# Splitting query and key projections: a whole copy by ScalarE and the first subtraction on GpSimd

## The chip, the cores and the metric

The kernel runs on one core of one Trainium2 chip. The metric is the device time of one execution in microseconds (us). The engines are called as in the profile: PE (TensorE; PEld are its weight loads), DVE (VectorE), ACT (ScalarE), POOL (GpSimd) and SP (SyncE, which issues most DMAs).

## The reference

A transformer layer in float32 on `x` of 16 items of 512 tokens and 256 features. After a layer norm `xn`, the output is `x + attention(xn) + experts(xn)`.

```
q, k = low_rank_proj(xn, q_a, q_b), low_rank_proj(xn, k_a, k_b)     # 16 heads of 16
att  = softmax(causal(q k^T / 4));  y = att v;  attention = y @ o_w.T + o_b
experts: 8 experts, each takes its top 128 tokens of an item by gate probability,
         silu(x_in w1) w2, scaled by the gate and added to their rows
```

## The kernel before, in words

The low-rank factors are folded into one weight per side at the start. To keep float32 accuracy with bf16 matmuls, every query and key projection is split into three bf16 parts (first, middle, last), whose sum is the f32 value. The parts are stacked by DMA into `qstk` and `kstk` (six DMAs per side and item, one per term of the product), so that one bf16 matmul of 96 rows gives a score.

The attention stage runs over 16 items; each item has four slots (`g` = 0 to 3, four heads each), and each slot ten units `t` = 0 to 9. `slot_steps(b, g)` writes one common order of steps by hand, from the tables `SUMS` and `PROJECTIONS`; an entry (t, kind, ahead, k) puts a step for item b + ahead into unit t, behind that unit's score work. Every engine walks the same list and does its own part of each step, in order, so a step that waits holds up all behind it on that engine. Semaphores with counted values join the engines. Two items form the body of a loop; the first pair and the last are written out, with `prologue_steps` ahead.

In unit t of slot G, PE makes the transposed scores `scoret` of slot G+1 (line 887, two PSUM banks in turn) and the scores of slot G+3 (line 866, three banks). ACT takes exp of `scoret` (565), POOL masks the diagonal (469), and DVE takes row maxima of the scores (719). The value products of slot G, `pv` (908), come in units 2 and 5; the first needs all ten masks made during the slot before, and PE waits there. In slot 1 the first scores of the next item begin; PE waits for that item's twelve stacking DMAs (863).

A projection for item b+2 has steps `qk_first` and `qk` (three matmul passes each, 776), k = 0, 1 for the queries and 2, 3 for the keys. Its bank is one of two `SHARED` banks, used in turn in the order of the units and freed by a counter `shared_done`. Then:

- ACT copies the bank to bf16 as the first part (537).
- DVE subtracts the first part from the bank into `rest`, f32 in SBUF, and frees the bank (`take_low`, 588; called at 695). `rest` has two buffers.
- In step `mid`, ACT copies `rest` to bf16 as the middle part (541), POOL subtracts it from `rest` into the last part (460), and behind k=1 and k=3 SP issues the six DMAs of a side (400).

`mid` of k=3 stands in the next item's slot 0 at t=1 (ahead 1), those of k=0, 1, 2 in slot 3. POOL's other work in the order: adding the output bias to `xres` in slot 2 at t=1 (477), which waits for that transfer, and small steps of the layer norm. Behind the attention stage comes the expert stage (from line 963), which the change leaves alone.

Of the kernel before, what the change touches and what calls it, by code (L numbers as in the profile page):

```python
# [5 lines left out]
B, T, D = 16, 512, 256  # L6
# [19 lines left out]
def unit_parts(t, transposed):  # L26
# [5 lines left out]
    for h, i in parts:  # L32
# [12 lines left out]
     (9, "qk_first", 2, 1)],  # L45
    [(0, "qk", 2, 1), (0, "mid", 2, 0), (1, "mid", 2, 1), (4, "qk_first", 2, 2), (6, "qk", 2, 2), (8, "mid", 2, 2),
     (8, "qk_first", 2, 3), (9, "qk", 2, 3)])

SUMS = (
# [6 lines left out]
def slot_steps(b, g):  # L56

    G = GB * b + g  # L60
    put = {t: [] for t in range(UN)}
    for t, kind, ahead, k in SUMS[g]:
        if G + ahead < NG:
            put[t].append((kind, G + ahead, k))
    last_values = b == B - 2
    if last_values and g == 0:
        put[0].append(("v", b + 1, 0))
        put[1].append(("v", b + 1, 1))
        put[3].append(("v", b + 1, 2))
        put[4].append(("v", b + 1, 3))  # L70
    for t, kind, ahead, k in PROJECTIONS[g]:
        if last_values and kind == "v":
            continue
        if 0 <= b + ahead < B and (kind, b + ahead) != ("mid", 1):
            put[t].append((kind, b + ahead, k))
    for t, step in routing_steps(G):
        put[t].append(step)
    out = []
    for t in range(UN):
        out += [("scoret", G + 1, t)] * (G + 1 < NG) + [("score", G + 3, t)] * (G + 3 < NG) + put[t]  # L80
    return out
# [28 lines left out]
def prologue_steps():  # L110

    foldt = lambda n: [("foldt", n, half) for half in range(2)]
    qk = lambda b, mt: [("qk_first", b, mt), ("qk", b, mt)]
    out = [("xload", 0, 0), ("lnstat", 0, 0), ("lnstat", 0, 1), ("lnapply", 0, 0), ("xload", 1, 0)]

    out += foldt(0) + [("fold", 0, 0)] + foldt(1) + [("xt", 0, 0), ("xt", 0, 1), ("fold", 1, 0)]
    out += foldt(2) + qk(0, 0) + foldt(3) + qk(0, 1)
    out += [("mid", 0, 0), ("fold", 2, 0), ("mid", 0, 1), ("fold", 3, 0), ("wv", 0, 0), ("wv", 1, 0)]
    out += [("lnstat", 1, 0), ("lnstat", 1, 1)] + qk(0, 2) + qk(0, 3)
    out += [("mid", 0, 2), ("v", 0, 0), ("mid", 0, 3), ("v", 0, 1), ("v", 0, 2), ("lnapply", 1, 0), ("v", 0, 3)]  # L120
    out += [("xt", 1, dt) for dt in range(DT)] + [("wo", dt, 0) for dt in range(DT)] + [("ob", 0, 0)]
    for t in range(UN):
        out.append(("score", 0, t))
        if t in (0, 2, 4, 6):
            out += qk(1, t // 2)
        if t in (2, 4, 6):
            out.append(("mid", 1, t // 2 - 1))
    for t in range(UN):
        out += [("score", 1, t)] + [("maxt", 0, 0)] * (t == 2) + [("maxd", 0, 0)] * (t == 3) + [("mid", 1, 3)] * (t == 4)
    for t in range(UN):  # L130
        out += [("scoret", 0, t), ("score", 2, t)] + [("maxt", 1, 0)] * (t == 3) + [("maxd", 1, 0)] * (t == 4)
    return out
# [28 lines left out]
def build(nc, x, q_a, q_b, k_a, k_b, v_w, v_b, o_w, o_b, choice_w, w1, w2, out):  # L161
    fp32, f32r, bf16 = mybir.dt.float32, mybir.dt.float32r, mybir.dt.bfloat16
    i32, u32 = mybir.dt.int32, mybir.dt.uint32
    ALU, ACT, AX = mybir.AluOpType, mybir.ActivationFunctionType, mybir.AxisListType
# [5 lines left out]
                                            "rankt", "rowst")]  # L170
    unit_of = {s: n for n, s in enumerate(shared)}

    split_of = {s: n for n, s in enumerate(s for s in shared if s[0] in ("fold", "wv", "wo", "xt", "qk", "yt"))}
    U_PAIR, S_PAIR = 48, 16
    for i in range(1, PAIRS - 2):
        for s, z in zip(pair_steps(i), pair_steps(i + 1)):
            assert s not in unit_of or unit_of[z] - unit_of[s] == U_PAIR
# [9 lines left out]
    with ctx:  # L187
        def sem(name):
            return ctx.enter_context(nc.semaphore(name))
# [28 lines left out]
        with ExitStack() as mem:  # L218
# [67 lines left out]
            shared_done = [sem(f"shared_done{u}") for u in range(2)]  # L286
            hi_done = sem("hi_done")
            mid_done = sem("mid_done")
            lo_done = sem("lo_done")
            stacked = [sem(f"stacked{u}") for u in range(2)]  # L290
            logit_done = sem("logit_done")
# [54 lines left out]
            def bank_of(step):  # L346
                return unit_of[step] % 2
# [5 lines left out]
            def emptied(step, at):  # L353

                return at(unit_of[step] // 2 + 1, U_PAIR // 2)
# [67 lines left out]
            def _(pool):  # L423
# [15 lines left out]
                def steps(todo, at):  # L439
                    for step in todo:  # L440
                        kind, n, k = step
                        if kind == "gather":
                            if n == 0:
                                pool.wait_ge(gate_step, GATED + RANK_OPS + 3)
                                pool.wait_ge(xn_stored, 16 * B)
                            gather(nc, moe, xn_dram, n)
                        elif kind == "lnstat" and k == 1:

                            pool.wait_ge(mv_done, at(n + 1, 2))
                            if n >= 1:  # L450
                                pool.wait_ge(xn_done, at(n, 2))
                            nc.gpsimd.tensor_tensor(vareps[:], meanvar[:, :, 1], eps[:], ALU.add).then_inc(vareps_done, 1)
                            pool.wait_ge(vareps_done, at(n + 1, 2))
                            nc.gpsimd.tensor_tensor(rstd[:], vareps[:], mhalf[:], ALU.pow).then_inc(rstd_done, 1)
                        elif kind == "mid":

                            pool.wait_ge(mid_done, at(GB * n + k + 1, 2 * GB))
                            if n >= 1:
                                pool.wait_ge(stacked[(n - 1) % 2], at(STACK_DMAS * ((n - 1) // 2 + 1), STACK_DMAS))
                            nc.gpsimd.tensor_tensor(qk_part[2][:, k, :], rest[k % 2][:], qk_part[1][:, k, :],  # L460
                                                    ALU.subtract).then_inc(lo_done, 1)
                        elif kind == "scoret":

                            pool.wait_ge(exp_done, at(UN * n + k + 1, 8 * UN))
                            pool.sem_inc(pool_past1, 1)
                            cols = [col // P for _, _, col, _ in unit_parts(k, True)]
                            unit = probs[n % 2][:, 512 * k:512 * k + 512].rearrange("p (a c) -> p a c", c=P)
                            block = unit[:, 0:1, :] if len(cols) == 1 else unit[:, 0:cols[1] + 1:cols[1], :]
                            nc.gpsimd.affine_select(out=block, in_=block, compare_op=ALU.is_ge, fill=0.0, base=0,  # L469
                                                    pattern=[[0, len(cols)], [1, P]], channel_multiplier=-1)\  # L470
                                .then_inc(causal_done, 1)
                        elif kind == "xres":
                            pool.wait_ge(xres_in, at(16 * (n + 1), 32))
                            if n == 0:
                                bias = ("ob", 0, 0)
                                pool.wait_ge(shared_done[bank_of(bias)], emptied(bias, at))
                            nc.gpsimd.tensor_tensor(xres[:], xres[:], ob_all[:].unsqueeze(1).to_broadcast([P, TT, D]),
                                                    ALU.add).then_inc(xres_done, 1)
# [4 lines left out]
            def _(act):  # L483
# [15 lines left out]
                def steps(todo, at):  # L499
                    for step in todo:  # L500
# [32 lines left out]
                        elif kind == "qk":  # L533
                            act.wait_ge(shared_ready[p], filled(step, at))
                            if n >= 1 and k == 0:
                                act.wait_ge(stacked[(n - 1) % 2], at(STACK_DMAS * ((n - 1) // 2 + 1), STACK_DMAS))
                            nc.scalar.activation(qk_part[0][:, k, :], src[:], ACT.Copy).then_inc(hi_done, 1)
                        elif kind == "mid":
                            qk = ("qk", n, k)
                            act.wait_ge(shared_done[bank_of(qk)], emptied(qk, at))  # L540
                            nc.scalar.activation(qk_part[1][:, k, :], rest[k % 2][:], ACT.Copy).then_inc(mid_done, 1)  # L541
                        elif kind == "v":
                            act.wait_ge(shared_ready[p], filled(step, at))
# [30 lines left out]
            def _(dve):  # L574
# [9 lines left out]
                def take_low(step, at, low, whole, high):  # L584

                    p = bank_of(step)
                    dve.wait_ge(hi_done, split(step, at))
                    nc.vector.tensor_tensor(low, whole, high, ALU.subtract).then_inc(shared_done[p], 1)

                def steps(todo, at):  # L590
                    for step in todo:
# [97 lines left out]
                            take_low(step, at, xt_lo[:, k, :], src[:], xt_hi[:, k, :])  # L689
                        elif kind == "yt":  # L690
                            take_low(step, at, yt_lo[:, k, :], src[:], yt_hi[:, k, :])
                        elif kind == "qk":
                            if 4 * n + k >= 2:
                                dve.wait_ge(lo_done, at(4 * n + k - 1, 8))
                            take_low(step, at, rest[k % 2][:], src[:], qk_part[0][:, k, :])
                        elif kind == "ob":

                            dve.wait_ge(weights_in, N_WEIGHTS)
# [483 lines left out]
```

## Time and profile before

| | |
|---|---|
| median of 3 runs | 1292.59 us (1291.87 to 1296.5) |
| profiled execution | 1295.71 us, of which the span of the trace is 1293.8 us |
| busy PE, DVE, ACT, POOL | 92%, 75%, 52%, 53% of the span |
| PE's granted clock | 0.969 of full speed, mean |

The attention stage lies from about 54 us to 850 us, the expert stage behind it. A busy time is the share in which an engine had an instruction running; the waits say which event ended an idle stretch. As each engine works in the order of one list, the place of a wait in that order says more than the share.

### The profile page before, as it was taken

The numbers are of one execution on the slowest core, as the hardware profiler recorded it, in microseconds if no ns is written. First come the engines' busy times: TensorE is split into PE (matmuls) and PEld (weight loads), VectorE is DVE, ScalarE is ACT, GpSimd is POOL, SyncE is SP. The second block draws the span as 40 slices with busy tenths as digits, with TensorE's granted clock in tenths as the row PEclk, the third lists the DMA queues.
The fourth block names the chain that finished last, engine by engine and source line by source line (L and its number), as shares of the span: only waits on it lengthen the run. The fifth ranks groups of instructions, "written<-read, shape, count | busy, mean of one in ns | idle before, by whom it ended". The sixth has DMA issues, their size and how long they took to land. (4 is left out here: it accounts for less than half of the span.)

```text
span 1293.8 us, 29459 instructions
## 1 busy us (share of the span) xinstructions
PE 1184.1 (92%) x8502; PEld 819.8 (63%) x8502; DVE 967.2 (75%) x3293; ACT 668.7 (52%) x1312; POOL 692.0 (53%) x1021
## 2 busy tenths in 40 slices
PE   6799999999999999999999998769999999999995
PEld 5545555555555555555555553348988888888885
DVE  3588888879889888888888879935666666666662
ACT  2357667667667677677667665522332323233320
POOL 1235344355355355345345443344888888888885
PEclk9779999999999999999999999979999999999998
DMA  5443443443443443443444342132555555556454
GB/s 141 114 116 83 116 116 100 116 116 98 115 115 98 115 115 99 115 115 100 113 115 112 100 99 67 34 114 38 111 99 95 114 93 102 94 100 109 85 78 53
DMA packets 106287, 130.31 MB, mean 101 GB/s; under 512 B 21580, under 2 KB 75476, under 8 KB 106196
## 3 DMA queue, kind: packets, MB, share of 16 engines
q1 hardware_dynamic: 76356, 94.46, 28.1%
q0 software_dynamic: 24576, 33.57, 15.6%
q10 hardware_dynamic: 5264, 1.32, 0.5%
q8 instruction: 27, 0.44, 0.1%
q14 instruction: 64, 0.52, 0.1%
HBM read 44.84 MB, written 33.55 MB: 61 GB/s over the span
## 5 line engine op out<-in xcount | busy, mean ns | idle before, releaser
L719 DVE CUSTOM_DVE_ANT_0 junk<-bank,rowmask 128x256 bf16<-128x256 f32 (+3 forms) x1024 | 454.9, 485 | 60.3 <-PE bank L866 38.0
L565 ACT ACTIVATE probs<-bank 128x512 f32<-128x512 f32 x640 | 377.3, 598 | 158.0 <-PE bank L887 143.8
L469 POOL TENSOR_SCALAR_AFFINE_SELECT probs<-probs 128x256 f32<-128x256 f32 (+1 forms) x640 | 224.2, 363 | 311.0 <-ACT probs L565 308.9
L866 PE MATMUL bank<-kstk,qstk 96*128 96x256 bf16 (+3 forms) x1024 | 250.7, 306 | 34.3 <-DVE rowmax L719 17.3
L887 PE MATMUL bank<-qstk,kstk 98*128 98x256 bf16 (+3 forms) x1024 | 251.0, 307 | 3.8 <-ACT probs L565 2.6
L1049 POOL DMA_INDIRECT out_rows<-mixed,rows x128 | 208.9, 1632 | 58.2 <-issue 38.1
L1078 ACT ACTIVATE hid<-bank 128x512 f32<-128x512 f32 x128 | 76.6, 598 | 228.5 <-PE bank L1141 228.5
L908 PE MATMUL bank<-probs,vaug 128*32 128x512 f32 (+3 forms) x2048 | 168.5, 448 | 6.6 <-POOL probs L469 6.6
L1157 PE MATMUL bank<-w_hi,hid_hi 128*128 128x256 f32 x512 | 147.3, 288 | 0.0
L1157 PE MATMUL bank<-w_hi,hid_lo 128*128 128x256 f32 x512 | 144.9, 283 | 0.0
L1157 PE MATMUL bank<-w_lo,hid_hi 128*128 128x256 f32 x512 | 144.8, 283 | 0.0
L866 PEld LDWEIGHTS bank<-kstk,qstk 96*128 96x128 bf16 x1024 | 89.7, 100 | 79.5 <-DVE rowmax L719 38.3
L887 PEld LDWEIGHTS bank<-qstk,kstk 98*128 98x128 bf16 x1024 | 76.7, 99 | 99.2 <-issue 48.0
L1109 DVE TENSOR_SCALAR mixed<-bank,gate_sel 128x256 f32<-128x256 f32 x128 | 56.1, 480 | 92.0 <-PE bank L1157 92.0
L908 PEld LDWEIGHTS bank<-probs,vaug 128*32 128x32 f32 x2048 | 54.1, 110 | 95.9 <-issue 74.1
L460 POOL TENSOR_TENSOR qk_part<-rest,qk_part 128x512 bf16<-128x512 f32 x64 | 74.6, 1166 | 58.0 <-ACT qk_part L541 55.1
L1157 PEld LDWEIGHTS bank<-w_lo,hid_hi 128*128 128x128 f32 x512 | 98.2, 192 | 0.0
L1157 PEld LDWEIGHTS bank<-w_hi,hid_hi 128*128 128x128 f32 x512 | 98.2, 192 | 0.0
L1157 PEld LDWEIGHTS bank<-w_hi,hid_lo 128*128 128x128 f32 x512 | 98.1, 192 | 0.0
L1098 DVE CAST hid_hi<-hid 128x512 fp32r<-128x512 f32 x128 | 56.9, 445 | 48.7 <-ACT hid L1078 47.1
L1100 DVE TENSOR_TENSOR hid_lo<-hid,hid_hi 128x512 fp32r<-128x512 f32 x128 | 89.2, 697 | 4.4
L719 DVE DVE_READ_ACCUMULATOR2_ANT rowmax<- 128x1 f32 x1024 | 84.8, 83 | 0.0
(131 smaller groups left out, 2097.8 us busy)
## 6 DMA issues: line engine op xcount, KB each, us to landing
qstk<-qk_part SPq DMA_DIRECT2D x96, 256.0 KB, 4.8
kstk<-qk_part SPq DMA_DIRECT2D x96, 256.0 KB, 4.7
xln<-in_L_attn_hidden_states SPq DMA_DIRECT2D x16, 512.0 KB, 6.1
xn_rows<-xn SPq DMA_DIRECT2D x16, 512.0 KB, 2.8
xres<-in_L_attn_hidden_states SPq DMA_DIRECT2D x16, 512.0 KB, 3.6
out_rows<-xres SPq DMA_DIRECT2D x16, 512.0 KB, 2.9
qstk<-in_L_ffn_w SPq DMA_DIRECT2D x8, 512.0 KB, 4.0
kstk<-in_L_ffn_w SPq DMA_DIRECT2D x8, 512.0 KB, 3.9
```

The costliest lines, as they stand in the source:

```text
L460: nc.gpsimd.tensor_tensor(qk_part[2][:, k, :], rest[k % 2][:], qk_part[1][:, k, :], ALU.subtract).then_inc(lo_done, 1)
L469: nc.gpsimd.affine_select(out=block, in_=block, compare_op=ALU.is_ge, fill=0.0, base=0, pattern=[[0, len(cols)], [1, P]], channel_multipli ...
L565: nc.scalar.activation(probs[n % 2][:, 512 * k:512 * k + 512], SCORET[k % 2][:], ACT.Exp, scale=SCALE).then_inc(exp_done, 1)
L719: last = nc.vector.tensor_tensor_reduce(out=junk[k % 2][:, col:col + width], in0=SCORE[score_bank(UN * n + k)][:, col:col + width], in1=ro ...
L866: last = nc.tensor.matmul(SCORE[score_bank(UN * n + k)][:, col:col + width], qstk[b % 2][0:KS, GH * g + h, P * i:P * i + P], kstk[b % 2][0 ...
L887: last = nc.tensor.matmul(SCORET[k % 2][:, col:col + width], kstk[b % 2][0:KS + SHIFT, GH * g + h, P * j:P * j + P], qstk[b % 2][0:KS + SH ...
L908: last = nc.tensor.matmul(Y[2 * HD * h:2 * HD * h + 2 * HD, P * k:T], vaug[b % 2][:, k, GH * g + h, :], probs[n % 2][:, col:col + width], ...
L1049: nc.gpsimd.indirect_dma_start(out=out_rows, out_offset=bass.IndirectOffsetOnAxis(ap=moe.rows[:, GB4 * grp + j, e:e + 1], axis=0), in_=mix ...
L1078: nc.scalar.activation(hid[k % 2][:], UP[k][:], ACT.Silu).then_inc(silu_done, 1)
L1098: nc.vector.tensor_copy(hid_hi[n % 2][:, k, :], hid[k % 2][:]).then_inc(hid_high, 1)
L1100: nc.vector.tensor_tensor(hid_lo[n % 2][:, k, :], hid[k % 2][:], hid_hi[n % 2][:, k, :], ALU.subtract).then_inc(hid_done, 1)
L1157: last = nc.tensor.matmul(DOWN[k][:, D * t:D * t + D], a, b, start=m == 0, stop=m == len(todo_mm) - 1)
```

## The change

ACT now makes two copies of each projection out of PSUM: the whole value in f32 into `rest`, and the first part in bf16; the second of them frees the bank. A new step `rest` makes POOL subtract the first part from `rest` in place, in SBUF. ACT's `mid` waits for that. DVE has no part in a projection any more. The tables are written anew: `qk_first` and `qk` come two units earlier for k=0 and k=2, one unit (or a slot's edge) earlier for k=1 and k=3, `mid` of k=1 and k=2 move by one unit, and `rest` is put in slot 2 at t=7 and slot 3 at t=0, 5 and 9.

```
-    [(0, "xt", 2, 0), (1, "xres", 0, 0), (1, "xt", 2, 1), (6, "qk_first", 2, 0), (8, "qk", 2, 0),
-     (9, "qk_first", 2, 1)],
-    [(0, "qk", 2, 1), (0, "mid", 2, 0), (1, "mid", 2, 1), (4, "qk_first", 2, 2), (6, "qk", 2, 2), (8, "mid", 2, 2),
-     (8, "qk_first", 2, 3), (9, "qk", 2, 3)])
+    [(0, "xt", 2, 0), (1, "xres", 0, 0), (1, "xt", 2, 1), (4, "qk_first", 2, 0), (6, "qk", 2, 0), (7, "rest", 2, 0),
+     (8, "qk_first", 2, 1), (9, "qk", 2, 1)],
+    [(0, "mid", 2, 0), (0, "rest", 2, 1), (2, "mid", 2, 1), (2, "qk_first", 2, 2), (4, "qk", 2, 2), (5, "rest", 2, 2),
+     (6, "qk_first", 2, 3), (7, "mid", 2, 2), (8, "qk", 2, 3), (9, "rest", 2, 3)])
...
-    qk = lambda b, mt: [("qk_first", b, mt), ("qk", b, mt)]
+    qk = lambda b, mt: [("qk_first", b, mt), ("qk", b, mt), ("rest", b, mt)]
...
+                        elif kind == "rest":          # POOL
+                            qk = ("qk", n, k)
+                            pool.wait_ge(whole_done, at(4 * n + k + 1, 8))
+                            pool.wait_ge(shared_done[bank_of(qk)], emptied(qk, at))
+                            nc.gpsimd.tensor_tensor(rest[k % 2][:], rest[k % 2][:], qk_part[0][:, k, :],
+                                                    ALU.subtract).then_inc(rest_done, 1)
...
-                            nc.scalar.activation(qk_part[0][:, k, :], src[:], ACT.Copy).then_inc(hi_done, 1)
+                            if 4 * n + k >= 2:
+                                act.wait_ge(lo_done, at(4 * n + k - 1, 8))
+                            nc.scalar.activation(rest[k % 2][:], src[:], ACT.Copy).then_inc(whole_done, 1)
+                            nc.scalar.activation(qk_part[0][:, k, :], src[:], ACT.Copy).then_inc(shared_done[p], 1)
                         elif kind == "mid":
-                            qk = ("qk", n, k)
-                            act.wait_ge(shared_done[bank_of(qk)], emptied(qk, at))
+                            act.wait_ge(rest_done, at(4 * n + k + 1, 8))
...
-                        elif kind == "qk":            # DVE
-                            if 4 * n + k >= 2:
-                                dve.wait_ge(lo_done, at(4 * n + k - 1, 8))
-                            take_low(step, at, rest[k % 2][:], src[:], qk_part[0][:, k, :])
```

## Rows read from the trace of the kernel before

**Rows 1.** The page's first part: busy time, share of the span, instructions.
```profile
PE 1184.1 (92%) x8502; PEld 819.8 (63%) x8502; DVE 967.2 (75%) x3293; ACT 668.7 (52%) x1312; POOL 692.0 (53%) x1021
```

**Rows 2.** Windows: slots 2, 3, 0, 1; length, busy per engine, PEclk, DMA share, GB/s.
```profile
396.60:407.35 10.75, 10.61 (x81) 5.64 (x79) 9.76 (x39) 7.25 (x15) 5.02 (x10) 1.00 0.29 99
407.35:418.51 11.16, 11.08 (x84) 5.92 (x82) 9.39 (x38) 8.90 (x18) 7.09 (x14) 1.00 0.56 128
418.51:429.95 11.44, 10.99 (x92) 6.41 (x91) 9.93 (x40) 8.78 (x22) 4.73 (x11) 1.00 0.70 154
429.95:444.34 14.39, 13.21 (x113) 9.18 (x114) 12.04 (x52) 8.07 (x18) 5.04 (x13) 1.00 0.23 73
```

**Rows 3.** Waits of 100 to 800 us: total us, times, longest.
```profile
PE bank L866 <- DVE rowmax L719: 12.1, 23, 1.3
PEld bank L776 <- DVE rest L588: 8.2, 14, 0.7
```

**Rows 4.** Timeline of SP: start, us, line, transfer, count; two items.
```profile
421.88 3.81 SPq L400 DMA_DIRECT2D kstk<-qk_part  x6
469.72 3.89 SPq L400 DMA_DIRECT2D kstk<-qk_part  x6
```

**Rows 5.** Timeline of PE and its loads at the first score of slot 1.
```profile
431.13 0.39 PE L866 MATMUL bank<-kstk,qstk 96*128 96x512 bf16 x1 [1.51 <-DMA kstk<-qk_part]
478.94 0.10 PEld L866 LDWEIGHTS bank<-kstk,qstk 96*128 96x128 bf16 x1 [0.22 <-DMA kstk<-qk_part]
```

**Rows 6.** Timeline of PE, slot 3 of two items.
```profile
406.76 0.40 PE L776 MATMUL bank<-xt_hi,wqk_lo 128*128 128x512 f32 x1
407.00 0.39 PE L887 MATMUL bank<-qstk,kstk 98*128 98x384 bf16 x2
...
407.45 0.38 PE L887 MATMUL bank<-qstk,kstk 98*128 98x256 bf16 x2
...
407.99 1.71 PE L908 MATMUL bank<-probs,vaug 128*32 128x512 f32 x16
...
415.64 0.50 PE L776 MATMUL bank<-xt_hi,wqk_hi 128*128 128x512 f32 x1
...
646.97 1.71 PE L908 MATMUL bank<-probs,vaug 128*32 128x512 f32 x16
```

**Rows 7.** Timeline of ACT, slot 3 and the start of slot 0.
```profile
407.20 0.60 ACT L537 ACTIVATE qk_part<-bank 128x512 bf16<-128x512 f32 x1 [0.31 <-PE bank L776]
...
417.85 0.60 ACT L537 ACTIVATE qk_part<-bank 128x512 bf16<-128x512 f32 x1 [0.37 <-PE bank L776]
...
419.48 0.60 ACT L565 ACTIVATE probs<-bank 128x512 f32<-128x512 f32 x1
419.96 0.64 ACT L541 ACTIVATE qk_part<-rest 128x512 bf16<-128x512 f32 x1
```

**Rows 8.** Timeline of POOL, the same slots.
```profile
402.74 2.37 POOL L477 TENSOR_TENSOR xres<-xres,ob_all 128x1024 f32<-128x1024 f32 x1 [5.32 <-DMA xres<-in_L_attn_hidden_states]
405.07 2.83 POOL L469 TENSOR_SCALAR_AFFINE_SELECT probs<-probs 128x256 f32<-128x256 f32 x9
...
420.68 1.17 POOL L460 TENSOR_TENSOR qk_part<-rest,qk_part 128x512 bf16<-128x512 f32 x1
...
641.98 2.38 POOL L477 TENSOR_TENSOR xres<-xres,ob_all 128x1024 f32<-128x1024 f32 x1 [5.51 <-DMA xres<-in_L_attn_hidden_states]
```

**Rows 9.** Lines 588 and 460 over the trace: ns min/median/max.
```profile
L588 DVE TENSOR_TENSOR rest<-bank,qk_part x64: 684/692/693, 27.8 to 753.2; 128x512 f32<-128x512 f32 x64
...
L460 POOL TENSOR_TENSOR qk_part<-rest,qk_part x64: 1152/1164/1222, 31.9 to 756.1; 128x512 bf16<-128x512 f32 x64
```

**Rows 10.** Timelines of POOL and DVE at the start, and DVE later.
```profile
42.64 2.34 POOL L460 TENSOR_TENSOR qk_part<-rest,qk_part 128x512 bf16<-128x512 f32 x2 [1.95 <-ACT qk_part L541]
...
42.75 3.02 DVE L672 TENSOR_SCALAR xn<-xln,meanvar,rstd 128x256 f32<-128x256 f32 x4
...
99.06 1.38 DVE L672 TENSOR_SCALAR xn<-xln,meanvar,rstd 128x256 f32<-128x256 f32 x4
```

More of the change, by code:

```diff
@@ L73, in slot_steps @@
             continue
-        if 0 <= b + ahead < B and (kind, b + ahead) != ("mid", 1):
+        if 0 <= b + ahead < B and (kind, b + ahead) not in (("mid", 1), ("rest", 1)):
             put[t].append((kind, b + ahead, k))
@@ L171, in build @@
     unit_of = {s: n for n, s in enumerate(shared)}
-    split_of = {s: n for n, s in enumerate(s for s in shared if s[0] in ("fold", "wv", "wo", "xt", "qk", "yt"))}
-    U_PAIR, S_PAIR = 48, 16
+    split_of = {s: n for n, s in enumerate(s for s in shared if s[0] in ("fold", "wv", "wo", "xt", "yt"))}
+    U_PAIR, S_PAIR = 48, 8
     for i in range(1, PAIRS - 2):
@@ L288, in build @@
             mid_done = sem("mid_done")
+            whole_done = sem("whole_done")
+            rest_done = sem("rest_done")
             lo_done = sem("lo_done")
```

## The prediction

> **What bounds the kernel now.** I read the shares of busy time first. They say PE 92%, DVE 75%, ACT 52%, POOL 53% [rows 1], which is a mean over an attention stage and an expert stage; the change touches the attention stage alone. So next come the windows of one batch item, slot by slot [rows 2]. In slots 2 and 3, where the projections of queries and keys are made, PE is busy for 10.61 of 10.75 us and 11.08 of 11.16; DVE has over 1 us to spare in each, ACT 3.5 and 2.3. Freed DVE time is therefore not freed kernel time. The waits over 700 us agree: PE's matmuls waited 12.1 us for DVE's row maxima, and the weight load of a projection waited 8.2 us for the subtraction that is to leave DVE [rows 3].
>
> Then I follow the transfer. Six stacking DMAs for kstk are issued at 421.88, and the first score of the next item starts at 431.13, after an idle 1.51; one item later they are issued at 469.72 and the score starts at 478.94 [rows 4, 5]. That is 9.25 and 9.22 us. Both times PE was waiting for it, and from issue to issue there are 47.84 us, the item's period. So the loop that sets the pace is: first score of slot 1, slots 1, 2 and 3 at PE's rate, the last `mid` in slot 0 (ACT, then POOL), the DMAs, the next first score. Whatever PE does in slot 0 behind that `mid` is hidden. A delay anywhere else in this loop costs its full length in each item.
>
> **What leaves DVE.** 64 subtractions of 0.692 us [rows 9], 44 us in all, off an engine that bounds nothing here. What they can give back is what waits for them. In slot 3 the projection of k=3 starts its first half at 415.64, where the load had nothing else to wait for than the subtraction of k=2 [rows 3, 6]: 8.2 us over 14 items is 0.58 each at the load, of which part lies beside the matmul before it. I take 0.35 per item as gained (bounds 0 and 0.58). PE's 12.1 us of waits for maxima are 0.5 us each [rows 3]; the first half of k=0, moved up to t=4 of slot 2, gives DVE time ahead of one of them, of which I put the gain at 0.3. But it lies ahead of the place of the next part, where POOL decides, so I count it at 0 (bound 0.3).
>
> **What POOL gets, and the wait behind it.** POOL's queue has the bias addition to xres in slot 2 at t=1. It waits 5.32 us for its transfer, and ends at 405.07; only then come the masks of slot 2 from t=2 on. Nine of them take 2.83 us, up to 407.90, the ninth being the first of slot 3 [rows 8]. The first value product of slot 3 needs the eighth and starts at 407.99 [rows 6], so the eighth, at about 407.55, is 0.44 us early. Of the 13 items with this pattern another stands in the rows: the addition ends at 644.36, the eighth mask 2.5 later at 646.85, and the value product starts at 646.97 [rows 6, 8], 0.1 early. I take 0.35 as the middle. The change puts the step `rest` of k=0 at t=7 of slot 2, in front of the masks of t=8 and t=9. Its price is not in the trace, since POOL does no such subtraction yet; the nearest row is the same operation with the same shape of f32 inputs and a bf16 output, 1.164 us [rows 9]. An f32 output could cost more or less: 0.9 to 1.5. I take 1.16. PE then waits 1.16 less 0.35: **+0.8 us** per item (bounds 0.5 and 1.4). Behind this wait stand, in PE's order, all of slot 3.
>
> **What ACT gets.** Two copies where there was one, 0.49 from start to start. After the projection of k=1, now in t=9 of slot 2, ACT does the whole copy, the first part, and only then the exp of t=0 in slot 3. PE's scoret of t=2 needs that exp (two banks in turn). The last pass now ends 0.16 after t=0's scoret starts, which is two units of 0.45 ahead of 407.45: 406.72. Copy at 406.76 (0.04 behind the pass, as at 407.20 behind 407.16), first part 407.25, exp 407.74 to 408.34 [rows 6, 7]. Scoret of t=2 would come 0.9 later than the 407.45 of now, or 0.6 with the closed gap of 0.3. This runs beside POOL's 0.8 and isn't added: the later one counts. The other places have room: `mid` of k=1 waits in ACT's queue for POOL's `rest` of k=1 at t=2, but PE is then in its value products for 1.7 us; in t=6 of slot 2 and t=4 of slot 3 the exp behind the copies is needed two units later or behind another value product.
>
> **The last `mid`.** Now ACT does the exp of t=1 in slot 0 at 419.48 and `mid` of k=3 at 419.96; POOL takes the rest from 420.68, and the DMAs go at 421.88 [rows 4, 7, 8]. In the new order the projection of k=3 ends one unit of 0.45 earlier (417.81, which is 0.04 ahead of the copy at 417.85, becomes 417.36), and ACT does whole copy 417.41, first part 417.90, exp of t=9 418.39 to 418.99. POOL masks it (0.1 to start, 0.31), and then does `rest` of k=3 for 1.16, to 420.56, while now DVE has it done before ACT comes to it. ACT's `mid` starts at 420.6 to 420.7 instead of 419.96, and POOL and the DMAs follow: **+0.7 us** per item. Bounds are 0 (if ACT is late anyway) and 1.1 (a slower `rest`, two masks ahead of the last one). This is in the loop and exposed.
>
> **The start.** Eight of the 64 projections are made ahead of the loops. The chain for kstk of item 0 has the extra copy and two POOL subtractions in a row behind one another: about 1.2 us more ahead of the first score, which waits for this transfer. Item 1's four subtractions leave DVE where its maxima set the pace, 0.6 each, of which about a half may show. Sum +0.5 (bounds -1.5 and +2).
>
> [...] At the start, the DVE row of four scalings for the layer norm of item 1 took 3.02 us beside two POOL subtractions; the same four later took 1.38 [rows 10]. [...]
>
> **The sum.** Per item 0.8 + 0.7 - 0.35 = 1.15 us. Items 0 to 13 make projections for the one two ahead, so 14 x 1.15 = 16.1, plus 0.5: 16.6 us. I cut this to 15, as some of the small parts will overlap. The profiled execution took 1295.71 us (span 1293.8), the median of the runs shown is 1292.59; 1295.71 + 15 = 1310.7, and against the median 1307.6, rounded **1308**.
>
> **Rivals.**
> *The earlier projections pay.* The projection of k=3 ends one step sooner, banks come free from ACT alone, and if ACT and POOL had time enough, 0.35 + 0.3 per item would be saved: 14 x 0.65 = 9 us, 1283.5. It decides at one point: `rest` of k=3 must be done before ACT's turn at 419.96, which needs POOL's subtraction below 0.5 us or the exp of t=9 0.7 us sooner; and the masks' 0.4 us of room in slot 3 must hold. ACT's spare 2.3 us in slot 3 speaks for it, the order of the queues against. 8%.
> *Delays and gains cancel.* POOL's f32 subtraction takes 0.9, exps slip in, the closed gap counts: 14 x 0.25 = 3.5, 1296. 16%.
> *ACT becomes the bound in slots 2 and 3.* ACT is busy 8.90 of 11.16 in slot 3; with two copies more and one moved out it comes to about 9.4, and each wait for POOL in its queue (`mid` of k=1 up to 1.5 us) is lost if it doesn't fit PE's value products. Then 2.2 us per item: 14 x 2.2 = 31, 1323. [...] 20%.
> *The forecast.* 56%.
>
> Against no change, about 0.5% (6.5 us, so 1286 to 1299) is what a measurement of this kernel can tell. Slower 0.76, same 0.16, faster 0.08. For the range: 1296 from the cancelling case, 1322 nearly up to ACT's.
>
> **What would show it.** In the new trace: value product of slot 3 started by POOL's mask, with PE idle 0.6 to 1 us ahead of it; DVE's busy time down by some 40 us and its share of idle up; POOL's `rest` at 1.16 us; from the first score of slot 1 to the DMAs for kstk 1.15 longer, and 9.2 from issue to score as now; period 49.0 instead of 47.8. I am wrong if that period is 47.8 or less, if the mask comes before PE is ready, or if ACT's last `mid` isn't preceded by a wait for POOL.

## The result, and the profile after

The changed kernel takes 1349.8 us (median of 4 runs, 1348.38 to 1354.3), the kernel before, run beside it, 1294.55. The ratio is 1.0425, 95% interval [1.0389, 1.0462]: 55 us slower, where 15 had been forecast. The sign was right and the size was wrong by more than three times. The profiled execution has a span of 1348.5 us against 1293.8, so the traces show the same 54.7 us.

The first part of the changed kernel's page, in the columns of [rows 1], and its line for GpSimd's new subtraction `rest` (463), in the columns of [rows 9]:

```profile
PE 1200.6 (89%) x8502; PEld 822.2 (61%) x8502; DVE 940.5 (70%) x3229; ACT 691.2 (51%) x1376; POOL 762.8 (57%) x1085
...
L463 POOL TENSOR_TENSOR rest<-rest,qk_part x64: 1142/1160/1188, 26.8 to 806.5; 128x512 f32<-128x512 f32 x64
```

POOL is 70.8 us busier and is still idle for 43% of the span; its subtraction takes 1.160 us, the price of the nearest row. PE is busy 16.5 us longer with the same 8502 matmuls, yet its share fell from 92% to 89%. So PE both waits more and works more slowly, and the time has to be found by position. Taking the issue times of kstk's DMAs, from the second on, as the milestones gives 14 intervals, which sum to 52.5 us more than before (2.3 more come behind the last). PE in these 14 intervals, before and then changed (from:to, length, busy, granted clock, DMA share, GB/s):

```profile
70.87:757.27 686.40, 659.32 (x5144) 0.99 0.42 108
70.79:809.74 738.95, 674.84 (x5142) 0.96 0.40 101
```

Length less busy is PE's idle time: 27.1 us before and 64.1 now. So 37.0 of the 52.5 us are waits of PE, and 15.5 are the same matmuls running at a lower clock. By interval they fall in three kinds:

| intervals | more than before |
|---|---|
| 7 that contain no jump back | 1.26 to 1.65 each, 10.1 together |
| 5 that contain the loop's jump back (every second item) | 6.2 to 7.9 each, 35.0 together |
| the first 2 | 4.7 and 2.8 |

**An interval of the first kind.** SP's and PE's timelines, the kernel before and then the changed one: the DMAs for kstk, the first score of slot 1, the first value product of slot 3, that of slot 0, and the next DMAs. "x1" is the part of a group of six that the window held.

```profile
565.37 0.55 SPq L400 DMA_DIRECT2D kstk<-qk_part  x1
574.59 0.39 PE L866 MATMUL bank<-kstk,qstk 96*128 96x512 bf16 x1
599.20 0.64 PE L908 MATMUL bank<-probs,vaug 128*32 128x512 f32 x4
611.69 0.64 PE L908 MATMUL bank<-probs,vaug 128*32 128x512 f32 x4
613.11 0.55 SPq L400 DMA_DIRECT2D kstk<-qk_part  x1
```

```profile
605.49 0.55 SPq L403 DMA_DIRECT2D kstk<-qk_part  x1
614.62 0.39 PE L874 MATMUL bank<-kstk,qstk 96*128 96x512 bf16 x1
640.21 0.64 PE L916 MATMUL bank<-probs,vaug 128*32 128x512 f32 x4
652.37 0.64 PE L916 MATMUL bank<-probs,vaug 128*32 128x512 f32 x4
654.52 0.55 SPq L403 DMA_DIRECT2D kstk<-qk_part  x1
```

The stretches before were 9.22, 24.61, 12.49 and 1.42 us; now they are 9.13, 25.59, 12.16 and 2.15. That is -0.09, +0.98, -0.33 and +0.73, where the forecast had 0, +0.8, -0.35 and +0.7. The sum is 1.29; the forecast was 1.15. This part was sized nearly right.

**The next interval**, 654.52 to 710.32, is 6.77 us longer than that one. PE's and ACT's timelines of the changed kernel, and PE's windows (length, busy, granted clock, DMA share, GB/s):

```profile
664.55 0.39 PE L874 MATMUL bank<-kstk,qstk 96*128 96x512 bf16 x1 [3.03 <-DMA kstk<-qk_part]
...
707.67 0.61 PE L895 MATMUL bank<-qstk,kstk 98*128 98x256 bf16 x2 [4.13 <-ACT probs L577]
```

```profile
701.82 0.60 ACT L577 ACTIVATE probs<-bank 128x512 f32<-128x512 f32 x1
707.02 0.60 ACT L577 ACTIVATE probs<-bank 128x512 f32<-128x512 f32 x1 [4.60 <-issue]
```

```profile
614.62:628.26 13.64, 13.64 (x117) 1.00 0.15 51
...
664.55:679.81 15.26, 15.26 (x116) 0.89 0.12 41
666.00:669.40 3.40, 3.40 (x23) 0.55 0.00 0
706.70:713.50 6.80, 5.83 (x26) 0.51 0.30 81
```

Two things stand there that no term of the sum had.

First, ACT stands still for 4.60 us with "issue" as the cause: nothing that the profile knows held it, yet the next instruction didn't start. It happens once per turn of the loop, at 289.05, 393.89, 498.71, 602.19 and 707.02 (4.44 to 4.64 us), always at the first instruction of the loop's body. PE then waits 4.13 for that exp. In the kernel before only DVE has such gaps (2.78 to 3.02, in the same five places). They make two of PE's first scores behind the jump late by 0.63 and 0.66 us, and in those items PE then doesn't wait for kstk:

```profile
470.89 0.39 PE L866 MATMUL bank<-kstk,qstk 96*128 96x512 bf16 x1 [0.63 <-DVE rowmax L719]
...
472.87 0.39 PE L866 MATMUL bank<-kstk,qstk 96*128 96x512 bf16 x1 [0.66 <-DVE rowmax L719]
```

Second, PE waits 3.03 us for kstk instead of 1.51 [rows 5], and within 1.5 us its granted clock drops to about half, 0.55 over the next 3.40 us. PE is busy throughout the stretch from the first score to the third value product, which takes 15.26 us instead of the 13.64 of one item earlier. Half clock stands around ACT's gap too (0.51 in the last window). Before, the clock was 1.00 in the windows of the item shown [rows 2].

The transfer itself takes longer as well: from the issue of kstk's DMAs to the score it is 10.03 us here, where it was 9.13 one interval earlier and 9.22 before.

### The profile page after: what moved, and what is told of

The parts are those of the page before. It is cut to its first block and busy times, and to the rows that moved or that the text cites. A ratio compares the mean times of both kernels' runs of the same rounds, so it can differ in the third digit from the quotient of the medians.

```text
span 1348.5 us, 29600 instructions
## 1 busy us (share of the span) xinstructions
PE 1200.6 (89%) x8502; PEld 822.2 (61%) x8502; DVE 940.5 (70%) x3229; ACT 691.2 (51%) x1376; POOL 762.8 (57%) x1085
## 3 DMA queue, kind: packets, MB, share of 16 engines
q10 hardware_dynamic: 5264, 1.32, 0.5%
## 5 line engine op out<-in xcount | busy, mean ns | idle before, releaser
L895 PE MATMUL bank<-qstk,kstk 98*128 98x256 bf16 (+3 forms) x1024 | 255.2, 312 | 38.2 <-ACT probs L577 34.1
L874 PE MATMUL bank<-kstk,qstk 96*128 96x256 bf16 (+3 forms) x1024 | 253.9, 310 | 38.4 <-DMA kstk<-qk_part 27.4
L916 PE MATMUL bank<-probs,vaug 128*32 128x512 f32 (+3 forms) x2048 | 179.6, 472 | 7.0 <-POOL probs L479 7.0
L463 POOL TENSOR_TENSOR rest<-rest,qk_part 128x512 f32<-128x512 f32 x64 | 74.2, 1160 | 39.7 <-ACT qk_part L550 39.6
L1149 PE MATMUL bank<-pt_hi,w_hi 128*128 128x512 f32 x256 | 81.4, 400 | 4.7 <-DVE pt_lo L1102 4.7
```

Source lines behind the costliest of these rows:

```text
L874: last = nc.tensor.matmul(SCORE[score_bank(UN * n + k)][:, col:col + width], qstk[b % 2][0:KS, GH * g + h, P * i:P * i + P], kstk[b % 2][0 ...
L895: last = nc.tensor.matmul(SCORET[k % 2][:, col:col + width], kstk[b % 2][0:KS + SHIFT, GH * g + h, P * j:P * j + P], qstk[b % 2][0:KS + SH ...
L916: last = nc.tensor.matmul(Y[2 * HD * h:2 * HD * h + 2 * HD, P * k:T], vaug[b % 2][:, k, GH * g + h, :], probs[n % 2][:, col:col + width], ...
L1149: last = nc.tensor.matmul(UP[k][:], a[:, dt, f], b[:, dt, :], start=m == 0 and dt == 0, stop=m == 2 and dt == DT - 1)
```

## The experiments

Theory A: ACT's gap at the back edge is a fetch of instructions. Theory B: the longer wait for kstk drops PE's clock. Rival C: neither matters beside the queues of ACT and POOL, which pay more than was estimated.

Two of the edits recur (shortened here), both on the loop over pairs of items, and leave its steps as they are. A *placed head* gives `head_slot` a number, 0 or in e2 239, as the position of the body's first instruction; a *hint* turns on `hint_back_edge` for the jump at the body's end. What either does to the gap at the jump is what the runs measure: with the head at 0 ACT's gap of 4.44 to 4.64 us is gone (e1), with the hint as well (e3), and with the head at 239 the kernel before gets one of 3.26 to 3.63 us (e2).

```
-                with eng.Fori(1, PAIRS - 1) as i:
+                with nc.Fori(1, PAIRS - 1, engines=[eng.engine], head_slot={ScalarE: 0}) as i:          # placed head
+                with nc.Fori(1, PAIRS - 1, engines=[eng.engine], hint_back_edge=True) as i:             # hint
```

### The back edge

**e1_after_head0**: the changed kernel, ACT's head placed at 0.

> [...] Theory: at each of five back edges ACT refetches its loop's first instructions, idle 4.6 us ("issue"), because its longer body no longer lies in what is held; with the head moved the idle goes, each of the five items that cost 6.2 to 7.9 us more than before costs 1.3, and the time falls by 28, to 1321. Rival: ACT waits there for data (a value product, yt) or for something DVE waits for too; then the idle 4.6 stays and the time is 1350.

Measured: 1340.9 (1334.07 to 1343.17), ratio 1.0363 [1.0341, 1.0386]. The five gaps are gone, but only 9 us came back, where the theory had 28. One gap stands where the loop is entered, and PE waited 3.06 us there:

```profile
185.93 0.60 ACT L578 ACTIVATE probs<-bank 128x512 f32<-128x512 f32 x1 [3.53 <-issue]
```

**e2_before_head239**: the kernel before, ACT's head placed at position 239.

> [...] Theory (refetch): ACT gets idle stretches of about 4.5 us ("issue") at the back edges that the kernel before does not have, 5 of them at 5 to 6 us each: 1294.5 + 28 = 1322. Rival (the idle comes from the added copies and waits): no such stretch, 1294.

Measured: 1320.75 (1317.84 to 1321.89), ratio 1.0195 [1.017, 1.0221]. ACT and PE at one of the five edges, timelines of this kernel:

```profile
477.65 0.60 ACT L566 ACTIVATE probs<-bank 128x512 f32<-128x512 f32 x1 [3.60 <-issue]
...
478.30 0.61 PE L888 MATMUL bank<-qstk,kstk 98*128 98x256 bf16 x2 [2.60 <-ACT probs L566]
```

With the same instructions and the same order, ACT's gap appears when the body is shifted, and each edge item takes 51.2 to 51.3 us instead of 47.8 to 49.4. The profile shows the fetches themselves: its pages count the packets of a DMA queue of the kind "instruction". The kernel before, the changed one, e1 and e2:

```profile
q14 instruction: 64, 0.52, 0.1%
...
q14 instruction: 85, 0.70, 0.2%
...
q14 instruction: 61, 0.50, 0.1%
...
q14 instruction: 91, 0.75, 0.2%
```

The packets are many where ACT has the gaps and few where it has none, and two or three of them start within each of these gaps, 1.3 to 2.2 us behind its beginning. Theory A is shown. One turn of ACT's loop is 291 instructions in the trace of the kernel before and 313 in the changed one. With the 22 more came a gap of 4.44 to 4.64 us per jump, and with the 291 moved to position 239 one of 3.26 to 3.63. From which length, and at which positions, a jump has to wait for a fetch is not shown.

**e3_after_hint**: the changed kernel, hint on ACT. **e8_both_heads**: e1 with DVE's head placed at 0 as well.

> [...] Theory (refetch): the idle 4.6 us of ACT at the back edges shrinks to under 1, and the time is 1321 to 1325. Rival (a wait for data): 1350.

> [...] DVE's idle 3.6 us at the back edge (3.0 in the kernel before) should go. Theory: now that the items are longer, that idle lies in part in front of the next maxima; items with an edge gain up to 1 us, 5 us in all, 1336. Rival: it is hidden behind the wait for kstk as in the kernel before, 1341.

Measured: e3 1339.43 (1338.95 to 1345.85), 1.0356 [1.0322, 1.039]; e8 1341.19 (1333.96 to 1343.44), 1.0336 [1.0279, 1.0394]. The hint takes ACT's gap away as well as the head did (60 packets of kind "instruction" for 85), but its theory's 1321 to 1325 was missed by 14: again about 10 us came back. In e8 the rival (1341) held. For DVE the placed head did nothing: 3.56 to 3.97 us stayed. One turn of DVE's loop is 574 instructions in the trace of the changed kernel, against ACT's 313; whether its length is the reason is not shown.

**e9_after_both_hints**, **e10_before_both_hints**: the hint on ACT and DVE, with the change and without.

> The changed kernel with the loop-back hint for ScalarE and VectorE. Theory (the back edges' refetch is hidden on both engines; what stays is 1.3 to 1.5 us in each item from the queues, plus what the half clock takes): 1318 to 1330, items even at 49 to 49.5 with no idle at the edges. Rival (VectorE's idle in the changed kernel is covered by the wait for kstk): as with ScalarE's hint alone, 1336 to 1342.

> The kernel before with the same hint. Theory (VectorE's idle of 2.8 to 3.0 us at the edges lies beside PE's wait for kstk, as in the trace of before, so nothing is won): 1290 to 1296. Rival (part of it is exposed): 1280 to 1288.

Measured: e9 1343.48 (1338.87 to 1347.98), 1.0374 [1.0338, 1.0409], above the expected band; e10 1298.44, 1.0025 [1.0012, 1.0038], 2 us above its theory. In both no engine has a gap at an edge any more, and still e9 is 45 us slower than e10. So taking the fetches away returns 6 to 10 us of the 55 and not the 35 that the table of intervals suggests. The items of e9 take 50 to 52 us, and none of them 49. Why is in its windows, 6 us behind five first scores in a row (same columns as above; the waits for kstk ahead of them were 2.41, 2.44, 2.51, 2.45, 2.41):

```profile
402.50:408.50 6.00, 6.00 (x37) 0.72 0.04 12
453.46:459.46 6.00, 6.00 (x37) 0.72 0.05 17
504.47:510.47 6.00, 6.00 (x37) 0.72 0.03 10
555.49:561.49 6.00, 6.00 (x46) 1.00 0.05 17
605.54:611.54 6.00, 6.00 (x31) 0.50 0.04 13
```

PE gets through 31 to 37 matmuls in six busy microseconds where it does 46 at full clock. Of the twelve waits from 196 to 759 us (2.41 to 3.19 us), 10 were followed by a stretch at half clock. In the changed kernel, the gap at the edge put PE so far behind that it didn't wait for the next transfer (its row at 614.62 has no idle before it); half clock came at the gap itself. Take the gaps away, and the wait for kstk, and with it mostly the half clock, comes in every item. PE in the 14 intervals of e9:

```profile
72.71:800.16 727.45, 675.52 (x5142) 0.96 0.40 103
```

Its idle time is 51.9 us, 12.2 less than in the changed kernel, though PE's five waits at ACT's gaps were 20.6 together. Its busy time is 675.5 against 674.8: the clock's loss is all still there. The gap had hidden waits for kstk of some 8 us.

### The clock

**d1_before_mid_late**: the kernel before, with one step one unit later, in slot 0.

```
-    [(0, "v", 1, 0), (1, "mid", 1, 3), (1, "yt", -1, 0), (2, "xload", 2, 0),
+    [(0, "v", 1, 0), (1, "yt", -1, 0), (2, "mid", 1, 3), (2, "xload", 2, 0),
```

> The kernel before with one step moved: `mid` of k=3 in slot 0 at t=2 instead of t=1. ScalarE's copy, GpSimd's subtraction and the DMAs come one unit, about 0.9 to 1.0 us, later; PE's wait for kstk goes from 1.5 to about 2.4. Theory (the longer wait drops the clock): 0.9 us of delay and 1.6 of half clock in most of 14 items, 2.3 each, 1322 to 1330, with a half-clock stretch behind most waits. Rival (the clock holds, only the delay shows): 14 x 0.9, 1305 to 1309.

Measured: 1322.95 (1320.48 to 1323.81), ratio 1.0203 [1.0181, 1.0225]. Theory B held, at the lower end of its range. Two first scores of this kernel, and its windows from each to the third value product:

```profile
440.17 0.39 PE L866 MATMUL bank<-kstk,qstk 96*128 96x512 bf16 x1 [2.60 <-DMA kstk<-qk_part]
...
490.98 0.39 PE L866 MATMUL bank<-kstk,qstk 96*128 96x512 bf16 x1 [1.32 <-DMA kstk<-qk_part]
```

```profile
440.17:455.38 15.21, 15.21 (x116) 0.89 0.15 52
490.98:504.60 13.62, 13.62 (x116) 1.00 0.13 45
```

The same 116 matmuls take 1.59 us more behind a wait of 2.60 than behind one of 1.32. From 240 to 745 us the waits were 2.56 to 2.62 in every second item, each followed by half clock, and 1.15 to 1.42 in the others, none followed by it; behind this stretch one of 1.30, at 791.24, was. The theory had expected half clock in most items, and it came in every second one. The rest of the loss is the delay itself: over the 14 intervals PE's idle time grew by 14.7 us and its busy time by 13.0 (41.8 and 672.4, against 27.1 and 659.3). One step of one copy cost 26 us.

The length of the wait alone doesn't decide. In e3 PE waits 1.40 to 1.56 us for DVE's maxima at the five edges, and four of these waits were followed by half clock.

**d2_after_k3_early**: the changed kernel with both hints, and k=2 and k=3 one unit earlier.

```
-    [(0, "mid", 2, 0), (0, "rest", 2, 1), (2, "mid", 2, 1), (2, "qk_first", 2, 2), (4, "qk", 2, 2), (5, "rest", 2, 2),
-     (6, "qk_first", 2, 3), (7, "mid", 2, 2), (8, "qk", 2, 3), (9, "rest", 2, 3)])
+    [(0, "mid", 2, 0), (0, "rest", 2, 1), (1, "mid", 2, 1), (1, "qk_first", 2, 2), (3, "qk", 2, 2), (4, "rest", 2, 2),
+     (5, "qk_first", 2, 3), (6, "mid", 2, 2), (7, "qk", 2, 3), (8, "rest", 2, 3)])
...                                             # and "mid" of k=3 first in slot 0, at t=0
```

> The changed kernel with the hint on both engines (1343 without more) and, in slot 3, the projections of k=2 and k=3 with their steps one unit earlier, `mid` of k=3 first in slot 0. Theory (the wait for kstk falls under 2 us, and the clock stays up): 1.0 of earlier DMAs and 1.6 of clock in each item, 1308 to 1318. Rival 1 (only the earlier DMAs show): about 1329. Rival 2 (ScalarE and GpSimd have no room for it in slot 3, the wait moves to there): 1338 to 1350.

Measured: 1308.31 (1307.05 to 1313.13), ratio 1.0096 [1.0066, 1.0127]: 35 us below e9, with all of the change's work still there. A first score, the window behind it, and a whole item:

```profile
534.50 0.39 PE L874 MATMUL bank<-kstk,qstk 96*128 96x512 bf16 x1 [0.97 <-DMA kstk<-qk_part]
```

```profile
534.50:540.50 6.00, 6.00 (x46) 1.00 0.08 29
...
525.25:573.85 48.60, 46.37 (x369) 1.00 0.42 109
```

No first score from 143 to 767 us is followed by half clock, and from 283 us on the items take 48.2 to 48.6, where e9's take about 51. The 14 intervals, in the columns of e9's row:

```profile
73.24:767.74 694.50, 656.63 (x5130) 0.99 0.42 107
```

Against e9 PE is busy 18.9 us less, which is clock, and idle 14.1 us less (37.9 against 51.9), which are the shorter waits. In e9 the waits were 2.41 to 3.19 us per item; here the longest of the 13 between 100 and 770 us are 1.57 and 1.66.

### The order and the split

**e4_order_only**: the kernel before, DVE still subtracting, with the new tables (without the steps `rest`). **e7_old_order_new_split**: the new split in the old tables, ACT's head placed; `rest` stands in slot 2 at t=9, slot 3 at t=0 and 7, and slot 0 at t=0.

> The kernel before with the new order of steps alone: projections and mid where the change puts them, but one copy by ACT and the subtraction by DVE out of PSUM. Theory: the order costs nothing, since what costs is ACT's second copy ahead of the exp of slot 3 and POOL's subtraction ahead of the last mid; the banks come free in time and the time is 1290 to 1294. Rival: the earlier projections themselves make the exp of t=0 in slot 3 late or put mid of k=1 off; then 5 to 10 us more, 1300 to 1305.

> The changed kernel's split (ScalarE's whole copy and first part, GpSimd's subtraction) in the order of the kernel before, with the head of ScalarE's loop body placed so that its back edge costs nothing. With the run that had the new order alone (1309, +15) and the one that had both with the head placed (1341, +46) this makes the fourth corner. Theory (order and split each cost their own, and add): 46 less 15, about 31 above before, 1326. Rival 1 (the split costs what it costs in either order, since GpSimd's subtraction and ScalarE's queue set the pace): 1338 to 1343. Rival 2 (the new order was needed for nothing and is most of the cost): under 1310.

Measured: e4 1309.45 (1307.38 to 1315.93), 1.0121 [1.0084, 1.0158]; e7 1414.04 (1411.34 to 1419.51), 1.0934 [1.0907, 1.0962]. Both are outside what was expected. The order alone costs 15 us, although no engine got more to do. But it isn't a separate term, since the split in the old order is 73 us worse than in the new (e1). Four waits of ACT in a single item of e7, all for POOL's `rest`, point to why; three of them:

```profile
631.32 0.63 ACT L553 ACTIVATE qk_part<-rest 128x512 bf16<-128x512 f32 x1 [0.51 <-POOL rest L463]
...
634.41 0.63 ACT L553 ACTIVATE qk_part<-rest 128x512 bf16<-128x512 f32 x1 [1.97 <-POOL rest L463]
...
644.40 0.63 ACT L553 ACTIVATE qk_part<-rest 128x512 bf16<-128x512 f32 x1 [1.25 <-POOL rest L463]
```

The old order puts `mid` where DVE, at 0.69 us, had the remainder ready. With POOL at 1.16 us and behind its masks, ACT stands before `mid`, and exps queue behind it. About half of the price is clock again: in the 14 intervals PE is idle for 91.3 us and busy for 713.9, against e1's 51.8 and 670.4. The order was what made the split bearable, and had its own price.

**e5_k1_behind_exp**: e1 with the second half of k=1's projection in slot 3 at t=0, behind the exp, so that ACT's copies don't delay it. **e6_k3_by_dve**: e1 with k=3 subtracted by DVE, as before.

```
-     (8, "qk_first", 2, 1), (9, "qk", 2, 1)],                 # e5
-    [(0, "mid", 2, 0), (0, "rest", 2, 1),
+     (9, "qk_first", 2, 1)],
+    [(0, "qk", 2, 1), (0, "mid", 2, 0), (0, "rest", 2, 1),
...
-                            nc.scalar.activation(rest[k % 2][:], src[:], ACT.Copy).then_inc(whole_done, 1)     # e6, for k=3
+                        elif kind == "qk" and k == 3:                                                          # DVE
+                            nc.vector.tensor_tensor(rest[k % 2][:], src[:], qk_part[0][:, k, :], ALU.subtract)
```

> The changed kernel with ACT's loop head moved, and the projection of k=1 finished in slot 3 at t=0, behind that unit's exp, as before the change, instead of in slot 2 at t=9. Theory: ACT's two copies ahead of the exp of t=0 hold up PE's scoret of t=2 by 0.9 us an item (seen as an idle 0.78); here that idle goes, 14 x 0.9 = 12 us, and a part of the half-clock stretches with it: 1341 becomes 1322 to 1329. Rival: POOL's rest of k=0 ahead of the masks then becomes the later one, and mid of k=1 waits longer; then the gain is under 5 us, 1336 to 1341.

> The changed kernel with ACT's loop head moved, and for k=3 alone the old split: one copy by ACT, the subtraction by DVE out of PSUM, no step rest. Theory: POOL's subtraction and the second copy make the last mid, and with it the six DMAs for kstk, 0.4 to 0.7 us late an item (ACT waits 0.40 for POOL there): 14 x 0.5 = 7, 1341 becomes 1334, and ACT's wait ahead of that mid is gone. Rival: that mid is set by PE's order alone; 1341.

Measured: e5 1342.98 (1339.46 to 1346.53), 1.0364 [1.0308, 1.042] against e1's 1.0363, so nothing was won, as the rival had it; e6 1332.26 (1322.22 to 1336.62), 1.0278 [1.0204, 1.0351], near its theory's 1334. PE at slot 3's first value product, the changed kernel and then e5; the wait ahead of them in the changed kernel is for ACT's exp, at `scoret` of t=2:

```profile
639.67 0.39 PE L895 MATMUL bank<-qstk,kstk 98*128 98x256 bf16 x2 [0.78 <-ACT probs L577]
...
640.21 0.64 PE L916 MATMUL bank<-probs,vaug 128*32 128x512 f32 x4
```

```profile
483.32 1.71 PE L917 MATMUL bank<-probs,vaug 128*32 128x512 f32 x16 [0.53 <-POOL probs L480]
```

ACT's two copies ahead of the exp and POOL's backlog are two paths with nearly one length. Relieve ACT's, and POOL's shows. Only taking a whole subtraction off (e6) seems to have helped, by about 9 us; its interval still touches e1's [1.0341, 1.0386].

### A faster kernel

If the loop that sets the pace ends in the last `mid`, moving that `mid` forward in the kernel before must help. **b3_mid_plain** does that alone; **b1_mid_early** has DVE's head placed at 0 too; **b2_mid_hint** has both hints instead.

```
-    [(0, "v", 1, 0), (1, "mid", 1, 3), ...
+    [(0, "mid", 1, 3), (0, "v", 1, 0), ...
...
-     (4, "qk_first", 2, 2), (6, "qk", 2, 2), (8, "mid", 2, 2), (8, "qk_first", 2, 3), (9, "qk", 2, 3)])
+     (2, "qk_first", 2, 2), (4, "qk", 2, 2), (6, "qk_first", 2, 3), (7, "mid", 2, 2), (8, "qk", 2, 3)])
```

> [...] Theory: the loop's pace is set by that last mid and the 9.2 us of its DMAs; they start 1 us earlier in relation to PE, and the bank wait of 0.35 goes: 14 x 1.3 = 18 less what PE's own work leaves, 1280 to 1285. Rival: the period is PE's and the wait for kstk only fills; then 1294.

> The kernel before, with VectorE's subtraction, with the projections of k=2 and k=3 two and one steps earlier, `mid` of k=2 one step earlier and `mid` of k=3 first in slot 0, and nothing else (the run of 1286 had VectorE's loop head placed as well). Theory (the last `mid` sits in the pace-setting loop, the head does little): 1285 to 1288, 7 us below before. Rival (it was the head): as before, 1292 to 1296.

> The same order, with the loop-back hint for VectorE and ScalarE in place of the placed head. Theory (the 2.2 to 2.4 us that VectorE still loses at each of 5 back edges are exposed by about 1.2 us there, and the hint fetches the target in time): five items fall from 48 to 49.6 to about 46.8 to 47.5, so 1279 to 1282. Rival (the hint does for VectorE no more than the head did): 1284 to 1289, with the idle still there.

Measured: b1 1286.22 (1284.2 to 1288.98), 0.9931 [0.9911, 0.9952], 1 us above its theory; b3 1285.96 (1282.64 to 1286.91), 0.9935 [0.992, 0.9951]; b2 **1274.04** (1269.74 to 1276.01), 0.984 [0.9821, 0.9859], 5 us better than expected. The head did nothing, the order gave about 8 us, and the hint 12 more; DVE's gaps of 2.17 to 2.40 us in b3 are gone in b2. The same hint won nothing in e10. DVE and PE at an edge of b3, PE's first score in b2, and an edge item's first score in e10:

```profile
459.50 0.69 DVE L719 CUSTOM_DVE_ANT_0 junk<-bank,rowmask 128x512 bf16<-128x512 f32 x1 [2.17 <-issue]
...
460.25 0.39 PE L866 MATMUL bank<-kstk,qstk 96*128 96x512 bf16 x1 [1.08 <-DVE rowmax L719]
```

```profile
509.39 0.39 PE L866 MATMUL bank<-kstk,qstk 96*128 96x512 bf16 x1 [0.46 <-DMA kstk<-qk_part]
```

```profile
479.01 0.39 PE L866 MATMUL bank<-kstk,qstk 96*128 96x512 bf16 x1 [1.85 <-DMA kstk<-qk_part]
```

In the kernel before, DVE's gap costs PE 1.3 us at the edge (0.63 and 0.66), and spares it the wait for kstk; without the gap (e10) PE waits 1.85 us for kstk there. With the wait down at 0.5, the gap spares PE nothing, and only then is the hint worth something. b2's items take 46.3 to 46.8 us in the loop, and it is 1.6% faster than the kernel before.

## Why the prediction was wrong

**What bounds it: right, with one reading too wide.** The loop through the last `mid` and the DMAs of kstk sets the pace; d1 and b3 show it in both directions. But PE was not waiting for kstk "both times": at 478.94 only its weight load had 0.22 us of idle, the matmul none, since DVE's gap at the edge had used up that item's wait. That a stall at the jump back can take the place of the wait for kstk could be seen there. That DVE lost 26.7 us of busy time (967.2 to 940.5, where some 40 had been forecast) bought nothing that shows.

**What leaves DVE: right.** -0.33 between the value products of slots 3 and 0, for -0.35 forecast, though no run singles out its cause.

**What POOL gets: near in size, wrong in engine.** +0.98 ahead of slot 3's value product, for +0.8. But the mask did not hold it, as had been named for the proof; ACT's path did, which the prediction had worked out at 0.6 to 0.9, "beside POOL's". e5 shows POOL's right behind it.

**The last `mid`: right.** +0.73 for +0.7, and ACT does wait for POOL's `rest` ahead of it, as its timeline shows:

```profile
652.62 0.63 ACT L553 ACTIVATE qk_part<-rest 128x512 bf16<-128x512 f32 x1 [0.40 <-POOL rest L463]
```

**The start: off, and small.** PE's timeline of the changed kernel puts the first score 1.1 us earlier than before (54.09 then), where +0.5 was forecast:

```profile
52.95 0.61 PE L874 MATMUL bank<-kstk,qstk 96*128 96x512 bf16 x1 [3.12 <-DMA kstk<-qk_part]
```

The four scalings of item 1 stand beside POOL subtractions again and take 3.96 us for 3.02 [rows 10]. That the subtractions are what lengthens them is not shown, and they cost the start nothing.

**Where it failed: the sum.** It held 1.15 us per item and nothing else, 16.1 us for 14 items. Measured were 52.5: 20.6 of them are PE's waits at ACT's gaps, 15.5 are PE's slower work, and the other 16.4 are further waits, which is what the forecast had. So the per-item term was nearly right, and the sum put two terms at nothing, the clock and the back edge.

- *The clock.* The steps' own delays lengthen the wait for kstk from 1.5 us to 2.4 to 3.1. The sum let PE keep the 1.00 of [rows 2]; behind a wait of 1.51 us that was so, and on a wait of 2.4 the row says nothing. A stretch at half clock costs 1.6 us each time (15.26 for 13.64; in d1 15.21 for 13.62). In the changed kernel's loop half clock follows three of the six waits of 2.9 to 3.1 us (not those at 247.56, 561.47 and 769.70) and stands at all five of ACT's gaps; in e9, 10 of 12 waits, which is 16 us, as much as all that was forecast. d2, with the change and without the long wait, runs at 1308, which is by chance the very forecast.
- *The back edge.* 22 more instructions in ACT's loop body brought ACT 4.4 to 4.6 us of fetching at each of five jumps, of which PE saw about 4. As it spares PE the next wait, removing it returned 6 to 10 us.
- *The transfer.* "9.2 from issue to score as now" held only in every second item; in those with the edge it was 9.89 to 10.06. The cause stays open. These DMAs are issued 10.1 us behind those of qstk, before 10.8, but a shorter distance doesn't explain it: in d2 it is 9.2 to 9.3 and the transfer takes 9.20 to 9.27 from 283 us on, in e9 it is 10.1 again and the transfer takes mostly 9.3 to 9.5.

These shares say where the time lies and not what each removal would give back: the gap takes the place of a wait for kstk, so that the 20.6 us at the gaps returned 6 to 10. e1, e3 and e9 bound the edge from one side, d2 the clock and the shorter waits together. The first two intervals (7.5 us, of which 4.8 are idle and 2.7 slower work) are taken apart by no run, and the 2.3 us behind the last milestone stay unexplained.

## What to carry to other kernels

Where PE waits once per item for a transfer, ask what PE's clock does when the wait grows: in d1 a wait of 2.60 us in place of 1.51 brought 1.59 us of slower work on top, and d2, with the steps one unit earlier, took 35 us less than e9. A clock of 1.00 at the present wait says nothing about a longer one (1.00 behind 1.32 us and 0.89 behind 2.60 in d1). In a looped kernel, count each engine's instructions in the body ahead of and behind the change: here a gap with "issue" at the first instruction of the body was a fetch, it came to an engine on the path with 22 instructions more (4.44 to 4.64 us with 313 a turn, none with 291), and a hint on the back edge removed it (e3). When one removed stall returns less than its length, look for the second that it was hiding.

## What the runs showed of the hardware

- ACT's gap at the back edge was 0 with a turn of 291 instructions where it stood by default (the kernel before), 3.26 to 3.63 us with the same body at position 239 (e2), 4.44 to 4.64 with 313 instructions (the changed kernel), and 0 again with those placed at 0 (e1, but 3.53 once, on entering the loop). A placed head at 0 left DVE's gap (574 instructions in the changed kernel) at 3.56 to 3.97 (e8); the hint removed it (e9).
- Half clock followed one of six waits for kstk of 1.47 to 1.53 us (the kernel before, from 230 to 720 us), one of six of 1.15 to 1.42 and all six of 2.56 to 2.62 (d1), three of six of 2.90 to 3.05 (the changed kernel) and 10 of 12 of 2.41 to 3.19 (e9); at 555.49 in e9 the clock stayed at 1.00 after 2.45. Behind waits of 1.40 to 1.56 us for DVE's maxima it followed in four of five (e3).
- The hints alone made the kernel before a little slower (e10: 1298.44 us, ratio 1.0025 [1.0012, 1.0038]).
